# A graph-attention kernel: the score shift between its two edge passes, with the mask prepared in the first stage, the scores transposed earlier, and the scans and clearing cut in pieces

## What is computed

```python
alpha = jnp.einsum('ehc,ehc->eh', q[dst], k[src] + e) / jnp.sqrt(32.)
m = jax.ops.segment_max(alpha, dst, num_segments=n)
p = jnp.exp(alpha - m[dst])
s = jax.ops.segment_sum(p, dst, num_segments=n)
w = p / (s[dst] + 1e-16)
out = jax.ops.segment_sum((v[src] + e) * w[:, :, None], dst, num_segments=n)
x = x + out + x_norm @ Wskip + mix(x_norm)
x = x + experts(layernorm(x))
```

## Time and profile before

| what | value |
|---|---|
| median of 3 runs | 3518.64 us (3511.38 to 3543.4) |
| the profiled execution: time | 3552.69 us |
| the profiled execution: span | 3550.9 us |
| mean granted clock of TensorE | 0.961 of full speed |
| busy, share of the span | PE 90%, DVE 79%, ACT 47%, POOL 46% |

### The profile page before, as it was taken

How to read it: one execution, slowest core, us unless ns; L and a number is a source line. 1 busy time by engine, 2 the same in 40 slices (tenths; PEclk the granted TensorE clock), 3 DMA queues, 4 the chain that set the end, 5 groups by cost and what they waited for, 6 DMA issues and landing times.

```text
span 3550.9 us, 72164 instructions
## 1 busy us (share of the span) xinstructions
PE 3186.8 (90%) x17312; PEld 2479.1 (70%) x17312; DVE 2793.7 (79%) x5687; ACT 1682.8 (47%) x4460; POOL 1646.0 (46%) x1803
## 2 busy tenths in 40 slices
PE   4997999999999999999999188888769999999999
PEld 3776666666666666666666155555569999999998
DVE  6775888888888888888887889999846666666665
ACT  1222333333333343333333256666546777777776
POOL 1223777777777777777775077777600000000000
PEclk9998899999999999999999599999979999999999
DMA  7345999899989899999998267777600000000000
GB/s 178 116 119 156 251 256 254 248 254 261 257 247 253 248 264 261 260 256 255 266 255 223 92 200 231 232 230 231 194 4 19 12 13 16 12 17 12 13 15 9
DMA packets 520909, 593.53 MB, mean 167 GB/s; under 512 B 187937, under 2 KB 396979, under 8 KB 520319
## 3 DMA queue, kind: packets, MB, share of 16 engines
q1 hardware_dynamic: 312408, 351.02, 34.0%
q0 software_dynamic: 201888, 232.77, 25.1%
q10 hardware_dynamic: 6409, 7.46, 0.7%
HBM read 426.91 MB, written 163.17 MB: 166 GB/s over the span
## 4 chain that ended last, share of the span: by engine, by line
PE 62%; DVE 12%; issue 8%; DMA 7%; SPq 3%; DVEq 3%; another core or an unknown queue 2%; ACT 1%; POOL 1%; ACTq 0%; POOLq 0%
PE psum L684 10%; PE psum L686 10%; PE psum L685 10%; PE psum L903 8%; PE psum L762 7%; PE psum L746 7%; PE psum L826 3%; DMA weights<-kv_tab,idx 3%; PE psum L817 2%; DVEq L1616 2%; DVE weights L1427 2%; DVE region_s L1613 1%; DVE part L1441 1%; DMA ve_d<-weights 1%
## 5 line engine op out<-in xcount | busy, mean ns | idle before, releaser
L625 POOL DMA_INDIRECT weights<-kv_tab,idx x450 | 549.1, 1220 | 254.5 <-issue 150.1
L762 PE MATMUL psum<-region_x,weights 125*125 x1800 | 493.3, 397 | 72.8 <-issue 39.7
L1183 ACT ACTIVATE region_s<-psum,bns 128x250 f32<-128x250 f32 x800 | 402.9, 554 | 287.8 <-PE psum L686 287.8
L746 PE MATMUL psum<-we,weights 64*125 64x256 f32 x1800 | 525.4, 410 | 0.0
L1665 DVE TENSOR_TENSOR parts_h<-region_s,parts_h 128x500 fp32r<-128x500 f32 x400 | 269.8, 679 | 311.2 <-ACT parts_h L1187 283.7
L903 PE MATMUL psum<-region_s 125*125 125x264 f32 x1800 | 452.5, 401 | 68.0 <-DVE region_s L1613 68.0
L1066 ACT ACTIVATE weights<-psum,region_s 125x250 f32<-125x250 f32 x450 | 211.3, 470 | 609.8 <-PE psum L754 289.0
L903 PEld LDWEIGHTS psum<-region_s 125*125 125x125 f32 x1800 | 304.6, 188 | 215.7 <-issue 76.9
L762 PEld LDWEIGHTS psum<-region_x,weights 125*125 125x125 f32 x1800 | 325.2, 191 | 177.3 <-issue 136.0
L625 POOL DMA_INDIRECT kv_more<-kv_tab,idx x300 | 370.4, 1235 | 126.9 <-issue 84.7
L746 PEld LDWEIGHTS psum<-we,weights 64*125 64x125 f32 x1800 | 298.5, 186 | 183.0 <-issue 155.2
(11 more groups left out here) (247 smaller groups left out, 7515.0 us busy)
## 6 DMA issues: line engine op xcount, KB each, us to landing
region_s<-ve_d SPq DMA_DIRECT2D x450, 256.0 KB, 3.0
ve_d<-weights SPq DMA_DIRECT2D x225, 256.0 KB
ve_d<-kv_more SPq DMA_DIRECT2D x150, 256.0 KB
weights<-in_attr_t SPq DMA_DIRECT2D x450, 62.5 KB
ve_d<-region_r SPq DMA_DIRECT2D x75, 256.0 KB
kv_tab<-region_s SPq DMA_DIRECT2D x50, 224.0 KB
region_s<-ab_d SPq DMA_DIRECT2D x450, 1.0 KB
weights<-kv_tab,idx POOLq DMA_INDIRECT x450
```

The lines of the kernel that those rows point to most:

```text
L625: nc.gpsimd.indirect_dma_start(kg[r][0:T, w, :], None, kv_tab, bass.IndirectOffsetOnAxis(idx[:, r, w:w + 1], 0)).then_inc(gathered[r], 16)
L746: last = mm(psum[0:T, s % 2, w * D:(w + 1) * D], att_b[:, s % RP, w * T:(w + 1) * T], we[:, :], start=True, stop=True)
L762: last = mm(psum[0:T, 2 + s % 2, w * D:(w + 1) * D], hott[:, s % RA, w * T:(w + 1) * T], q_all[:, bass.ds(j, 1), :].rearrange("p o d -> p ...
L1183: last = fn(fh[:, layer, o, :], psum[:, bk + e % 2, o * BN:(o + 1) * BN], ACT.Relu, bias=bns[:, layer, 1, col:col + 1], scale=bns[:, layer ...
```

## The change

- Stage A: POOL's queue loads five things with `dst_c_in` in place of one: `dst_c`, each row's predecessor (`dst_before`, 1 and 124 single numbers), and the first and last target of each chunk (`ends_i`, twice 128 single numbers). DVE makes the mask there, on 125x800 in bf16, with three more instructions, and SP stores it to `mask_d`.
- SP loads the mask 8 times replicated in three parts (2501, 2501 and 1250 elements of bf16 in 128 rows): part 0 before the steps of stage B, part 1 after the last read of the edge features, part 2 after the last store of values.
- PE does one part of the last block (`turn1`), then the 50 transposes, then the rest of it; ACT copies before it does its four parts of it.
- DVE: five forward scans of 1250, each when its ten tiles are copied, three backward ones, the ends; then the mix parts `sum2` and `stats2`; then `fence`; then `norm2`, `gain2` and `add2`; then three forward scans, and five times a backward scan of 1250 with its subtraction, from the last piece to the first.
- ACT takes the exponential of a piece and then copies its ten tiles. POOL clears the accumulator piece by piece, and DVE clears the last 1250.
- `sc_f` moves beside `sc_a` in `region_x`, so that SP starts the value loads of stage D without a wait for `exped`.
- The experts' weights: `w_x2` is loaded on SP after the last product of the mix branch, `w_xo` after two pieces are shifted, `w_x1` on ACT's queue after its last copy.

```diff
+PIECES = tuple(reversed(range(CT // CP)))
+PARTS = ((0, 2 * CP * T), (2 * CP * T, 4 * CP * T), (4 * CP * T, CE))
-        sc_m = region_x[:, CE:2 * CE + 1]
-        sc_f = region_s[:, 0:CE]
+        sc_f = region_x[:, CE:2 * CE]
+        sc_m = [weights[:, at:at + (hi - lo) // 2 + 1].bitcast(BF16)[:, 0:hi - lo + 1] for at, (lo, hi) in zip((1728, 0, 8192), PARTS)]
...
@@ SP, stage A
+            sp.wait_ge(mask_ready, 1)
+            sp.dma_start(mask_d.rearrange("(p n) -> p n", p=T), mask_c).then_inc(ab_out, 16)
@@ SP, around stage B
+            load_mask(0)
             each(NB, b_body)
             for s in range(LAGV):
                 store_ve(STEPS - LAGV + s, SB - LAGV + s)
             load_skip(NB - 2)
-            sp.wait_ge(score_done, STEPS)
+            sp.wait_ge(e_done, STEPS)
+            load_mask(1)
             for r in range(RK):
                 sp.wait_ge(ve_stored[r], 16 * (STEPS // RK))
...
+            load_mask(2)
...
-                sp.wait_ge(carried, 1)
...
-            sp.wait_ge(exped, CT // CP)
+            sp.wait_ge(m_y, NB)
+            load_experts(sp, 1, "w_x2")
+            store_mix(sp, NB - 1)
+            sp.wait_ge(shifted, 2)
+            load_experts(sp, 2, "w_xo")
@@ POOL
+                pool.dma_start(dst_before[0:1], dst_rows[0:1, 0:1]).then_inc(dst_c_in, 16)
+                pool.dma_start(dst_before[1:T], dst_rows[0:T - 1, ET - 1:ET]).then_inc(dst_c_in, 16)
+                for i, at in enumerate((0, CE - 1)):
+                    pool.dma_start(ends_i[:, i:i + 1], dst_chunks[:, at:at + 1].unsqueeze(1).broadcast_to((CH, H, 1))).then_inc(dst_c_in, 16)
...
-            pool.wait_ge(back, CT)
-            nc.gpsimd.memset(acc[:, NT // 2:NT, :], 0.0).then_inc(acc_zero, 1)
+            pool.wait_ge(score_done, STEPS)
+            clear(2 * CE, NT * PV)
+            for n, i in enumerate(PIECES[:-1]):
+                pool.wait_ge(back, (n + 1) * CP)
+                clear(i * CP * T, (i + 1) * CP * T)
+                pool.wait_ge(shifted, n + 2)
+                cleared = clear(CE + i * CP * T, CE + (i + 1) * CP * T)
+            cleared = clear(CE, CE + CP * T)
+            cleared.then_inc(acc_zero, 1)
@@ PE
-            for g in (*late_at.values(), *last_at.values()):
-                mix(NB - 1, 0, g)
+            mix(NB - 1, 0, late_at[1])
...
+            for g in (*list(late_at.values())[1:], *last_at.values()):
+                mix(NB - 1, 0, g)
@@ ACT
+            for g in late_at.values():
+                mix(NB - 1, g)
+            for n, i in enumerate(PIECES):
+                act.wait_ge(shifted, n + 1)
                 piece = sc_a[:, i * CP * T:(i + 1) * CP * T]
                 fn(piece, piece, ACT.Exp, scale=SCALE).then_inc(exped, 1)
+                for j in range(CP):
+                    act.wait_ge(back, n * CP + j + 1)
+                    copy(sview[:, i * CP + j, :, 0:H], ...).then_inc(back_out, 1)
+            act.wait_ge(m_y, NB)
+            act.dma_start(wx[0]..., a["w_x1"]...).then_inc(c_ff, 16)
@@ DVE, stage A
+            order(tt(mask_c[:, 0:1], dst_c[:, 0:1], dst_before, ALU.is_equal))
+            order(tt(mask_c[:, 1:ET], dst_c[:, 1:ET], dst_c[:, 0:ET - 1], ALU.is_equal))
+            ts(mask_c, mask_c, BIG, -BIG, ALU.mult, ALU.add).then_inc(mask_ready, 1)
@@ DVE, between the passes
+            for i in range(CT // CP):
+                lo, hi = i * CP * T, (i + 1) * CP * T
+                dve.wait_ge(mask_in[(0, 0, 1, 1, 2)[i]], 16)
+                dve.wait_ge(turned_out, (i + 1) * CP)
+                scan_on(lo, hi, sc_a, -BIG)
+            for lo, hi in reversed(PARTS):
+                scan_back(lo, hi, sc_a, -BIG)
...
+            for lo, hi in PARTS:
+                scan_on(lo, hi, sc_a, ends[:, 4:5])
+            for i in PIECES:
+                lo, hi = i * CP * T, (i + 1) * CP * T
+                scan_back(lo, hi, sc_f, ends[:, 5:6])
+                tt(sc_a[:, lo:hi], sc_a[:, lo:hi], sc_f[:, lo:hi], ALU.subtract).then_inc(shifted, 1)
             dve.wait_ge(back, CT)
-            order(nc.vector.memset(acc[:, 0:NT // 2, :], 0.0))
-            dve.wait_ge(acc_zero, 1)
+            order(nc.vector.memset(region_x[0:T, 0:CP * T], 0.0))
             d_body(0)
+            dve.wait_ge(acc_zero, 1)
```

More of the change, by code:

```diff
@@ L508, in b_body, with load_mask @@
                         load_mix(b + 1, 1 - u)
+            def load_mask(part):
+                lo, hi = PARTS[part]
+                n = min(hi + 1, CE) - lo
+                with nc.allow_non_contiguous_dma(reason="replicates the mask over the heads"):
+                    sp.dma_start(sc_m[part][:, 0:n], mask_d.rearrange("(c n) -> c n", c=CH)[:, lo:lo + n].unsqueeze(1).broadcast_to((CH, H, n))
+                                 ).then_inc(mask_in[part], 16)
+            load_mask(0)
             each(NB, b_body)
@@ L513, in _, with load_experts @@
             load_skip(NB - 2)
-            sp.wait_ge(score_done, STEPS)
+            sp.wait_ge(e_done, STEPS)
+            load_mask(1)
             for r in range(RK):
                 sp.wait_ge(ve_stored[r], 16 * (STEPS // RK))
[L518 to L526, removed]
-                sp.wait_ge(carried, 1)
-                for i, name in enumerate(("w_x1", "w_x2", "w_xo")):
-                    sp.dma_start(wx[i].rearrange("p e c n -> p (e c) n"),
-                                 a[name].rearrange("(k p) n -> p k n", p=128)).then_inc(c_ff, 16)
-            sp.wait_ge(exped, CT // CP)
+            load_mask(2)
+            store_mix(sp, NB - 2)
+            load_skip(NB - 1)
+            def load_experts(eng, i, name):
+                eng.dma_start(wx[i].rearrange("p e c n -> p (e c) n"), a[name].rearrange("(k p) n -> p k n", p=128)).then_inc(c_ff, 16)
+            sp.wait_ge(m_y, NB)
[3 more added lines that the diff above has]
+            load_experts(sp, 2, "w_xo")
             def d_body(it):
@@ L881, in _ @@
             mm(psum[:, 6, 0:2 * CH], to_rows, fence[:, 8:10, :].rearrange("p k c -> p (k c)"), start=True, stop=True).then_inc(ends_moved, 1)
[L883 to L889, removed]
+            pe.wait_ge(turned_out, CT)
+            for n in range(CT):
+                if n % CP == 0:
+                    pe.wait_ge(exped, n // CP + 1)
+                wait(pe, back_out, n - 3)
+                bt = PIECES[n // CP] * CP + n % CP
+                tr(psum[0:T, n % 4, 0:128], sc_a[:, bt * T:(bt + 1) * T], ident[:, :]).then_inc(back, 1)
             def sums(k, s, it):
@@ L1528, in _ @@
             order.reset()
[L1532 to L1539, removed]
@@ L1540, in _, with mask @@
-            last.then_inc(mask_ready, 1)
-            dve.wait_ge(mask_ready, 1)
-            order(ts(sc_m[:, 1:CE], sc_m[:, 1:CE], BIG, -BIG, ALU.mult, ALU.add))
-            for g in [*late_at.values(), *last_at.values()]:
-                mix(NB - 1, (NB - 1) % 2, g)
-            order.reset()
-            dve.wait_ge(turned_out, CT)
+            order(nc.vector.tensor_copy(ends[:, 2:4], ends_i))
+            scan = nc.vector.tensor_tensor_scan
+            def mask(lo, hi, back=0):
+                part, (at, end) = [(sc_m[i], p) for i, p in enumerate(PARTS) if p[0] <= lo and hi <= p[1]][0]
+                return part[:, lo - at + back:hi - at + back]
```

82 lines of the change are left out of this document (44 added, 38 removed).

## The result

| | before | after |
|---|---|---|
| median, 20 runs each, in turns on the same chip | 3529.78 us (3511.38 to 3546.07) | 3499.89 us (3484.07 to 3522.43) |
| the profiled execution: time | 3552.69 us | 3496.55 us |
| the profiled execution: span, granted clock | 3550.9 us, 0.961 | 3493.6 us, 0.967 |

The ratio is 0.9921 (95% interval 0.9903 to 0.9939). That is 28 us less than before, with 21 to 34 us as the interval (the two medians themselves lie 29.9 us apart): 0.8% faster, within the 1% named in the prediction. The forecast said 34.9 less.

What follows compares the result with a forecast made beforehand. It took the 119.05 us between last score and stage D, where engines take turns, as the source of all gain: -36.4 + 0.5 (stage B) + 1.0 (stage D) = -34.9 us, from 3518.6 to 3484 us, range 3470 to 3504.

Steps and rivals of the forecast that it cites:

- The stretch between the passes: From the last score to stage D's first sums: 82.6 us in place of 119.05, 36.4 less.
- a piece each: Last loop before stage D: DVE's backward scan of 1250 plus its subtraction, 4.18 us per piece, five times.
- ten tiles back: Transposing one piece's ten tiles back on PE, with ACT's copies partly hidden: 2.6 us, between 1.8 warm and 3.05 cold.
- from the last copy to stage D's first sums: Stage D's opening: `w_x1` issue 1.24 us, register load 1.52, first product and wait 1.2, one-hot tiles 0.6, and 0.3.
- PE is done with the mix branch before `sum2`: Mix branch's last block, moved behind the transposes on PE, stays hidden under DVE's scans with 2 to 3 us spare.
- 1 (the way back bound by PE and ACT): Rival: cold transposes set the last loop at 4.8 us; with `w_x1`'s full 4 us, -29, 3490 us; chance 0.17.
- 2 (clears block scans): Rival: POOL's clears block DVE's scans in the last loop, +8, so -27, 3492 us; chance 0.04.
- 3 and 4 (another price of a bf16 mask): Rivals on DVE's scans: bf16 mask speeds them, 3458 us, chance 0.03; or slows them, up to 3537, chance 0.03.
- 5 (the mix branch late): Rival: mix branch ends late on PE, so DVE's `sum2` waits 5 us; -30, 3489 us; chance 0.08.
- Stages A and B: Extra small loads and mask making in A: 0, at most 1.5 us; early mask load at B's opening: 0.5, at most 3.5.
- Stage D's start, "I take 1, nearer to the slots": `w_x1` beside the value loads makes them 4 us late, with six slots of 1.1 us in hand: 1 us lost.
- main branch: The forecast itself for the whole kernel: -34.9 us to 3484 us, own range 3478 to 3490; chance 0.65.

Runs made afterwards that it cites:

- e5: Changed kernel with the accumulator cleared as before, half each by POOL and DVE after the last transposes: 3528.76 us, stretch 86.8, stage D 519.4.
- e1: The kernel before, unchanged, profiled a second time: 3547.2 us, stretch between the passes 118.2, stage D 511.8.
- e12: Kernel before with small padding instructions on DVE, POOL and ACT, so stage D's loops begin where the changed kernel's do: 3506.86 us, stage D 519.4.
- e9: Changed kernel without one superfluous ACT wait at stage B's start, restoring ACT's old loop place: stage D 518.8 us; ratio 0.9931 to before.
- e10: Kernel before with one small ACT copy more, so ACT's stage D loop starts at 3361 as in the changed kernel: 3548.86 us, stage D 512.1.
- e4: Changed kernel with DVE's wait for the cleared accumulator ahead of stage D's first iteration, as before: 3518.11 us, stage D 520.1.
- e2: Changed kernel with two one-element DVE clears ahead of stage D, moving its loop's start in DVE's stream: 3515.12 us, stage D 519.0.
- e3: Changed kernel with 18 one-element DVE clears ahead of stage D, moving its loop's start in DVE's stream: 3516.47 us, stage D 518.4.
- e6: Changed kernel with three idle POOL clears after the last transposes, so POOL starts stage D late: 3521.12 us, stage D 522.7.

## Why the prediction came out as it did

**The stretch between the passes** was forecast at 82.6 us and took 82.1. The order of the steps was that of the forecast. The terms, in its own words:

| term | forecast | measured |
|---|---|---|
| first forward scan after the last score | 2.8 | 2.9 |
| a scan of 1250, of 2500 | 2.75, 5.35 | 2.82, 5.43 |
| third scans begin after the last score | 39 | 39.3 (1946.56) |
| subtraction of a piece, to the next start | 1.39 | 1.38 |
| a piece each | 4.18 | 4.23 |
| last subtraction ends after the last score | 73.4 | 74.3 |
| ten tiles back | 2.6 | 2.63 to 2.66 on PE, 2.35 on ACT |
| last copy ends after the last subtraction | 4.3 | 4.3 |
| ACT's issue of `w_x1` | 1.24 | 0.41 |
| from the last copy to stage D's first sums | 4.9 | 3.4 |
| PE is done with the mix branch before `sum2` | 2 to 3 | 1939.43 - 1934.0 = 5.4 |

The scans were each 1.5 to 2.5% low, and with the small work between them 0.9 us together. The subtraction was right: its row says 1.46 us now, but so it did before, where the prediction divided the time of five back to back by five (shortest, median and longest ns):

```profile
L1589 DVE TENSOR_TENSOR region_x<-region_x,region_s x5: 1455/1455/1464, 2024.2 to 2029.7; 128x1250 f32<-128x1250 f32 x5
```

Back to back the next instruction starts 1.37 us after it there, and 1.38 in the changed kernel (1963.20 to 1964.58). Stage D's opening was 1.5 us high, of it 0.8 the issue on ACT. The forecast's 1.24 was the mean of SP's two issues in the earlier trace rows, of 0.40 and 2.02 us; in the changed kernel SP's two take 0.40 and 0.39, and ACT's 0.41. That 1.5 and the 0.9 nearly cancel, which is luck. The cover of the mix branch was larger than forecast because its first 16 products, which had been slow at 6.27 us, took 3.55 behind the transposes. The granted clock was 0.57 of full speed in those 6.27 us, and 1.00 in the changed kernel, where the 50 transposes had kept PE busy since the last score. And the undone parts cost about what was expected of them: 15.6 us for the order on PE (16 to 17), 7.0 for the copies (5.5 to 8), 4.7 for the clearing (3.5), 2.4 for the early mask (1 to 4). They make 29.7 of the 37.0 us. The rest was not undone by itself; it is argued to be the mask and the mix branch, which DVE no longer has to do ahead of its first scan.

**The rivals.** 1 (the way back bound by PE and ACT) didn't come, but by little. Each exponential starts 0.03 to 0.04 us after its subtraction ends (1967.42 + 1.46 = 1968.88, then 1968.92), as the first one does, for which ACT had stood 37.91 us; so DVE sets the 4.23. But ACT's own round of exponential, wait for PE and copies is 1.24 + 0.67 + 2.35 = 4.26: it has no slack left, so a faster scan should meet ACT at once (no run tried it). The rival's premise was right: the granted clock is 0.50 through the whole way back, with the products in bursts of ten, about 1.5 us apart, where it was 0.68 before. The row of that stretch:

```profile
1964.00:1986.00 22.00, 13.26 (x50) 11.69 (x50) 17.54 (x10) 17.51 (x55) 9.96 (x9) 0.50 0.50 167
```

Rival 1 was priced at -29, with `w_x1`'s full 4 us in it. That is next to the measured -28 by chance: neither the slower loop nor the late values took place. 2 (clears block scans) is out by e5. 3 and 4 (another price of a bf16 mask) are out: (5.43 - 2.82) / 1250 = 2.09 ns for each element, against 2.08 before. By the Trainium skill (DVE: opcode table, instruction layouts, handler registers and perf-mode slots, Perf-mode slots) a two-source instruction with an f32 operand isn't doubled, and the trace agrees. 5 (the mix branch late) is out with 5.4 us to spare.

**Stages A and B** were 0 and +0.5. A is 325.6 us, between before's 327.2 and e1's 322.8. B's opening shows at most 0.8. Neither can be told from nothing.

**Stage D's start, "I take 1, nearer to the slots",** is the weak step. Its sum of transfers was right in kind: the first 10 us with `w_x1` move 326 GB/s at a share of 0.99. Before:

```profile
2050.67:2060.67 10.00, 9.79 (x29) 7.19 (x30) 7.29 (x15) 4.28 (x16) 6.01 (x10) 0.70 0.59 166
```

After:

```profile
1989.29:1999.29 10.00, 9.31 (x31) 7.00 (x32) 7.78 (x15) 5.84 (x22) 8.04 (x16) 0.81 0.99 326
```

But PE makes 31 products in them, not 29: the slots cover `w_x1`. It shows no cost later either, since e12, which loads it early, has the same stage D (519.4 against 519.2). In its place stage D lost 6.4 to 7.4 us by something that no term had, a slower rhythm of all its iterations, and e12 shows that the kernel before loses the same when its loops only begin at other places of the streams. With it the sum is -37.0 + 6.4 = -30.6; the forecast of -34.9 had +1.5 for stages B and D in place of +6.4, and 0.6 too little gain in the stretch. The measured -28 (21 to 34) holds the first and not the second. So the forecast's main branch was right on the stretch, and that the result lies within 1% is owed to a loss that nothing in the prediction names: 37 us alone would be 1.05% of the median before.

**Open** is which stream it is, and why. ACT's alone is excluded by e9 and e10; DVE's and POOL's were moved together only, in e12. The slow kernels have DVE's loop at 5947, 5948 (e4, e5), 5949 (e2) and 5965 (e3), and POOL's at 1536, 1527 (e5) and 1540 (e6); the fast ones have 5933 and 1523 alone. So a multiple of 16 or 32 instructions from DVE's old start does not bring the old rhythm back, and if it is POOL, four instructions (1523 to 1527) are enough to lose it. DVE's one-hot step has two inputs in SBUF and lies beside POOL's compares, which read it; the Trainium skill (SBUF — State Buffer, Who interferes with whom) says that such a pair block each other. So a shift of the one against the other within a step could be what the 45 ns are made of. No run here separates that, and no version with POOL's old place and the new order was tried. The finding itself rests on one trace of e12 against three of kernels with the old places (before, e1, e10).

## What to carry to other kernels

In a stretch where engines take turns, write down each engine's start and end from the trace and move whatever waits for nothing: 37 us of 119 went though no scan, subtraction or copy got faster, and the durations of scans and subtractions could be forecast to within 3%. Divide the time of a group back to back by its count, and don't compare that with the duration in a single row. Cut a serial scan only where a neighbour can start on the piece; a cut cost 0.3 us (five pieces took 14.35 us, from 1910.11 to 1924.46, where one scan took 13.15), and the overlap gave 7 us for the copies alone. Then compare the long stages that were not touched as well, by their events: here 75 iterations of unchanged work gave back 6 to 7 of the 37 us, and a padded copy of the kernel before is the experiment that finds such a thing.

## What the runs showed that was not expected

- A loop of identical instructions on five engines ran 1.4% slower (519.4 us in e12 against 512.1 in e10) when one-element instructions ahead of it moved where it begins in the streams of DVE and POOL.
- Stage B takes 1554 to 1611 us in 14 profiles in which its loop is the same, while no other stage spreads by more than 5 us between kernels with the same code in it, so most of the spread of this kernel's time is stage B's.
- The row of a DVE clear of 6600 elements begins 1.38 to 1.39 us late (before, e5, e10, e12: POOL's clear, which waits for the same transposes, begins that much earlier) and then lasts 5.56 us. So its whole price is 6.9 us, and not 5.56.
